# Latent attention: low half of the probabilities on GpSimd, query halves a step later, last score tile before the value matmuls

## What is computed

```python
q_blhd = jnp.einsum('bld,dhk->blhk', x_bld, Wq)
latent_bll = jnp.einsum('bld,dc->blc', x_bld, Wkv_down)
k_blhd = jnp.einsum('blc,chk->blhk', latent_bll, Wk_up)
v_blhd = jnp.einsum('blc,chk->blhk', latent_bll, Wv_up)
attn = jnp.einsum('bqhd,bkhd->bhqk', q_blhd, k_blhd) / jnp.sqrt(jnp.asarray(HD, dtype=x_bld.dtype))
attn = jax.nn.softmax(jnp.where(mask, attn, neg_inf), axis=-1)
y_blhd = jnp.einsum('bhqk,bkhd->bqhd', attn, v_blhd)
return jnp.einsum('bqhd,hdo->bqo', y_blhd, Wout)
```

## Time and profile before

| what | value |
|---|---|
| median of 3 runs | 2997.37 us (2995.15 to 2999.2) |
| profiled execution | 3000.29 us |
| its span on the core | 2998.6 us, mean granted TensorE clock 0.919 |
| busy in the whole span | PE 83%, DVE 72%, ACT 50%, POOL 28% |
| stretch of the latent attention's steps | 1918.66 to 2718 us |

### The profile page before, as it was taken

One profiled execution on the slowest core, in us unless ns is written; L12 is line 12 of the kernel. 1 busy time (PEld: TensorE's weight loads), 2 busy tenths in 40 slices (PEclk: granted clock), 3 DMA queues, 4 the chain that ended last, 5 costly groups with the idle time before them and its releaser, 6 DMA issues. The chain is left out here.

```text
span 2998.6 us, 38823 instructions
## 1 busy us (share of the span) xinstructions
PE 2496.2 (83%) x13889; PEld 1335.8 (45%) x13889; DVE 2165.9 (72%) x3838; ACT 1512.2 (50%) x2213; POOL 841.5 (28%) x820
## 2 busy tenths in 40 slices
PE   6999999999899989899991576688888888885256
PEld 3444444444444444344440344355555555554134
DVE  3389688878889887979107564688878978873765
ACT  5655554546455545555551121377766766772111
POOL 3444343544444434444440000102211211221000
PEclk9999999999999999999995776799999999997678
DMA  5000000000000000000001001000000000001001
GB/s 162 24 1 1 1 1 1 1 1 1 1 1 1 1 1 1 1 1 1 1 1 48 15 1 36 1 2 2 2 3 2 2 3 2 1 2 49 14 1 57
DMA packets 29459, 33.07 MB, mean 11 GB/s; under 512 B 6568, under 2 KB 25704, under 8 KB 29272
## 3 DMA queue, kind: packets, MB, share of 16 engines
q1 hardware_dynamic: 28296, 28.02, 2.9%
q0 software_dynamic: 976, 2.56, 0.3%
HBM read 25.72 MB, written 4.19 MB: 10 GB/s over the span
## 5 line engine op out<-in xcount | busy, mean ns | idle before, releaser
L716 POOL TENSOR_TENSOR g_lo<-g_full,g_hi 128x512 f16<-128x512 f32 x512 | 658.4, 1289 | 912.0 <-ACT g_hi L788 910.4
L788 ACT ACTIVATE g_full<-hid,b_col 128x512 f32<-128x512 f32 x512 | 351.4, 686 | 562.1 <-PE hid L152 560.6
L150 PE MATMUL hid<-y_hi,w_hi 128*128 128x512 f16 x1024 | 396.3, 387 | 37.6 <-DVE y_lo L774 34.9
L151 PE MATMUL hid<-y_lo,w_hi 128*128 128x512 f16 x1024 | 395.7, 386 | 0.0
L152 PE MATMUL hid<-y_hi,w_lo 128*128 128x512 f16 x1024 | 395.2, 386 | 0.0
L150 PE MATMUL acc<-g_hi,w_hi 128*128 128x512 f16 x1024 | 389.2, 380 | 0.0
L151 PE MATMUL acc<-g_lo,w_hi 128*128 128x512 f16 x1024 | 389.1, 380 | 0.0
L152 PE MATMUL acc<-g_hi,w_lo 128*128 128x512 f16 x1024 | 388.9, 380 | 0.0
L788 ACT ACTIVATE g_hi<-hid,b_col 128x512 f16<-128x512 f32 x512 | 348.6, 681 | 0.0
L2027 DVE TENSOR_REDUCE mla_m_col<-mla_ps 128x1 f32<-128x512 f32 (+3 forms) x512 | 225.2, 484 | 66.1 <-PE mla_ps L1869 60.0
L2130 ACT ACTIVATE mla_p_full<-mla_ps 128x1280 f32<-128x1280 f32 x128 | 158.3, 1237 | 143.8 <-PE mla_ps L1899 143.5
(11 more groups left out here) (369 smaller groups left out, 4781.6 us busy)
## 6 DMA issues: line engine op xcount, KB each, us to landing
stage<-in_L_ffn_w_dram SPq DMA_DIRECT2D x16, 512.0 KB, 4.9
x<-in_L_attn_x_dram SPq DMA_DIRECT2D x8, 512.0 KB, 8.4
routed_w<-in_L_ffn_w_dram SPq DMA_DIRECT2D x4, 1024.0 KB, 8.5
out_dram<-x SPq DMA_DIRECT2D x8, 512.0 KB, 5.7
mla_sums<-mla_sum_row SPq DMA_DIRECT2D x128, 2.0 KB
mla_wq<-in_L_attn_Wq_dram SPq DMA_DIRECT2D x1, 1024.0 KB, 6.8
mla_wout<-in_L_attn_Wout_dram SPq DMA_DIRECT2D x1, 1024.0 KB, 9.1
routed_wqkv<-in_L_ffn_wq_dram SPq DMA_DIRECT2D x2, 256.0 KB, 3.7
```

The lines of the kernel that those rows point to most:

```text
L150: pe.matmul(out, w_hi, v_hi, start=first, stop=False)
L151: pe.matmul(out, w_hi, v_lo, start=False, stop=False)
L716: pool.tensor_tensor(g_lo[:, g, :], g_full[:, g, :], g_hi[:, g, :], ALU.subtract).then_inc(tail_done, 1)
L788: act.activation(out[:, g, :], hid[:, ht % 4, :], ACT.Gelu, bias=b1_col[:, ht:ht + 1], scale=1.0 / WS).then_inc(gelu_done, 1)
```

## The change

Four things are changed, all in the steps of the latent attention:

- p_lo = p_full - p_hi goes from VectorE to GpSimd, as the first thing in its step. GpSimd's o_lo and norm columns stand behind it.
- ScalarE writes p_hi first and p_full second, with a semaphore for each (`p_head`, `p_whole`). TensorE's value matmuls do all products with p_hi first (waiting for `p_head`) and the four products with p_lo behind them (waiting for `p_tail`).
- The fourth score tile is issued right behind the key scores, ahead of the value matmuls, and VectorE takes its maximum right behind the other three.
- VectorE makes the query halves of an even step in the odd step behind it, after the maxima, but stays in the even step where the odd one uses bank 6 for a transpose (steps 4, 6 and 8, as long as there is a batch after).

```diff
-                    pe.wait_ge(exp_done, 2 * hn)
+                    pe.wait_ge(p_whole, hn)
...
                 last.then_inc(st_done, 1)
+
+
+            hb, hh, hn = head_of(b, h + LEAD - 2)
+            if exists(hb):
+                pe.wait_ge(s_max, TILES * hn + 1)
+                query_scores(pe, (slot + (h + LEAD - 2) // H) % 2, hh, QUERY_TILES[-1]).then_inc(s_rest, 1)
...
-                pe.wait_ge(p_tail, n + 1)
+                pe.wait_ge(p_head, n + 1)
...
+                own_cols = [slice(KEY_AT[t], KEY_AT[t] + SEQ - t * P) for t in range(TILES)]
                 for t in range(TILES):
-                    out = ps[:, own_bank, t * P:]
-                    cols = slice(KEY_AT[t], KEY_AT[t] + SEQ - t * P)
-                    hi, lo = p_hi[:, h % 2, cols], p_lo[:, h % 2, cols]
+                    out, hi = ps[:, own_bank, t * P:], p_hi[:, h % 2, own_cols[t]]
                     pe.matmul(out, val_hi[:, slot, t, :], hi, start=(t == 0), stop=False)
-                    pe.matmul(out, val_hi[:, slot, t, :], lo, start=False, stop=False)
-                    last = pe.matmul(out, val_lo[:, slot, t, :], hi, start=False, stop=(t == TILES - 1))
+                    pe.matmul(out, val_lo[:, slot, t, :], hi, start=False, stop=False)
+                pe.wait_ge(p_tail, n + 1)
+                for t in range(TILES):
+                    last = pe.matmul(ps[:, own_bank, t * P:], val_hi[:, slot, t, :], p_lo[:, h % 2, own_cols[t]],
+                                     start=False, stop=(t == TILES - 1))
...
+        def turn_bank_used(b, h):
+
+            return exists(b + 1) and h in (*TURN_AT, VALUE_AT)
+
+        def query_halves(dve, b, h):
+
+            hb, hh, hn = head_of(b, h + LEAD)
+            if not exists(hb):
+                return
+            for i in range(2):
+                ring = (hh + i) % RING
+                own = slice(i * LATENT, (i + 1) * LATENT)
+                dve.wait_ge(q_head, hn + i + 1)
+                dve.tensor_copy(q_hi[LATENT:P, ring, :], q_hi[0:LATENT, ring, :]).then_inc(q_twin, 1)
+                if i == 1:
+                    dve.wait_ge(q_twin, hn + i + 1)
+                dve.scalar_tensor_tensor(q_lo[0:LATENT, ring, :], ps[own, 6, :], 1.0 / WS, q_hi[own, ring, :],
+                                         ALU.mult, ALU.subtract).then_inc(q_tail, 1)
...
                 for t in QUERY_TILES[:-1]:
                     query_maxima(dve, hh, t)
+                dve.wait_ge(s_rest, hn + 1)
+                query_maxima(dve, hh, QUERY_TILES[-1])
+            if h % 2 == 1 and not turn_bank_used(b, h):
+                query_halves(dve, b, h - 1)
...
+            if h % 2 == 0 and turn_bank_used(b, h + 1):
+                query_halves(dve, b, h)
...
-                for out in (p_full, p_hi):
+                for out, made in ((p_hi, p_head), (p_full, p_whole)):
                     act.activation(out[:, hh % 2, :], flat[:, 3 * 512:3 * 512 + KEY_COLS], ACT.Exp,
-                                   scale=float(MLA_DIM) ** -0.5).then_inc(exp_done, 1)
+                                   scale=float(MLA_DIM) ** -0.5).then_inc(made, 1)
...
+            hb, hh, hn = head_of(b, h + 1)
+            if exists(hb):
+                pool.wait_ge(p_whole, hn + 1)
+                pool.tensor_tensor(p_lo[:, hh % 2, :], p_full[:, hh % 2, :], p_hi[:, hh % 2, :],
+                                   ALU.subtract).then_inc(p_tail, 1)
```

More of the change, by code:

```diff
@@ L1806, in latent_attention_layer @@
         st_done = sem("st_done")
-        exp_done = sem("exp_done")
+        p_head = sem("p_head")
+        p_whole = sem("p_whole")
         p_tail = sem("p_tail")
@@ L1974, in tensor_step @@
                     pe.wait_ge(x_added, TILES * before + h - OUTPUT_AT)
+                own_cols = [slice(KEY_AT[t], KEY_AT[t] + SEQ - t * P) for t in range(TILES)]
                 for t in range(TILES):
-                    out = ps[:, own_bank, t * P:]
-                    cols = slice(KEY_AT[t], KEY_AT[t] + SEQ - t * P)
-                    hi, lo = p_hi[:, h % 2, cols], p_lo[:, h % 2, cols]
+                    out, hi = ps[:, own_bank, t * P:], p_hi[:, h % 2, own_cols[t]]
                     pe.matmul(out, val_hi[:, slot, t, :], hi, start=(t == 0), stop=False)
-                    pe.matmul(out, val_hi[:, slot, t, :], lo, start=False, stop=False)
-                    last = pe.matmul(out, val_lo[:, slot, t, :], hi, start=False, stop=(t == TILES - 1))
+                    pe.matmul(out, val_lo[:, slot, t, :], hi, start=False, stop=False)
[3 more added lines that the diff above has]
+                                     start=False, stop=(t == TILES - 1))
                 last.then_inc(pv_done, 1)
-            hb, hh, hn = head_of(b, h + LEAD - 2)
-            if exists(hb):
-                pe.wait_ge(s_max, TILES * hn + 1)
-                query_scores(pe, (slot + (h + LEAD - 2) // H) % 2, hh, QUERY_TILES[-1]).then_inc(s_rest, 1)
             hb, hh, hn = head_of(b, h + LEAD)
@@ L2098, in vector_step @@
                                   ALU.subtract).then_inc(val_out, 1)
-            hb, hh, hn = head_of(b, h + LEAD - 2)
-            if exists(hb):
-                dve.wait_ge(s_rest, hn + 1)
-                query_maxima(dve, hh, QUERY_TILES[-1])
-            hb, hh, hn = head_of(b, h + 1)
-            if exists(hb):
-                dve.wait_ge(exp_done, 2 * (hn + 1))
-                dve.tensor_tensor(p_lo[:, hh % 2, :], p_full[:, hh % 2, :], p_hi[:, hh % 2, :],
-                                  ALU.subtract).then_inc(p_tail, 1)
-            hb, hh, hn = head_of(b, h + LEAD)
-            if exists(hb) and h % 2 == 0:
-                for i in range(2):
-                    ring = (hh + i) % RING
-                    own = slice(i * LATENT, (i + 1) * LATENT)
-                    dve.wait_ge(q_head, hn + i + 1)
-                    dve.tensor_copy(q_hi[LATENT:P, ring, :], q_hi[0:LATENT, ring, :]).then_inc(q_twin, 1)
-                    if i == 1:
-                        dve.wait_ge(q_twin, hn + i + 1)
-                    dve.scalar_tensor_tensor(q_lo[0:LATENT, ring, :], ps[own, 6, :], 1.0 / WS, q_hi[own, ring, :],
-                                             ALU.mult, ALU.subtract).then_inc(q_tail, 1)
+            if h % 2 == 0 and turn_bank_used(b, h + 1):
+                query_halves(dve, b, h)
         def scalar_step(act, b, slot, h):
```

## The result

The changed kernel took 3012.3 us in the median (3008.0 to 3014.2), the kernel before 2996.8 on the same chip: a ratio of 1.0048 (1.0036 to 1.0059), slower, where 2962 us was forecast. The profiled execution has a span of 3010.6 us. It is the shortest middle batch of the kernel before, not a typical one: over the six middle batches the mean is 104.4 us before and 108.0 with the change.

The account below looks back on a forecast made before the run. TensorE was taken as nearest the bound, VectorE close behind. Batch steps summed to 97.7 against 101.3 us; with all batches and 4 us of clock, 35 us off 3000.3 gave 2965, median 2962, range 2935 to 2993.

Parts of the forecast that it names:

- Steps 15, 1 and 3: Odd steps that wait for maxima: forecast to go to 4.0, 4.0 and 4.1 us.
- step 4: Its spread waits 1.4 us for ScalarE's evacuations, delayed by the later query halves; the step becomes 6.6 us.
- step 11: Its output waits 0.6 us for the last o_lo behind a p_lo on GpSimd, taking back the step's gain.
- about 2.6 us blocked: Step 8: VectorE's key casts and subtraction run into GpSimd; halves ready at 11.7 us instead of 9, step 9 grows 1.3.
- A: Rival: p_lo on GpSimd takes 4.2 us, so low products stall; kernel slower at 3042 us; chance 0.13.
- B: Rival: GpSimd and VectorE hardly contend for SBUF, so turns and step 9 come earlier; 2930 us; chance 0.15.
- C: Rival: ScalarE's queue eats the gain, every spread step waiting as step 4 does; 2991 us; chance 0.12.
- the signs that I had named: Changed profile: among others p_lo 2.6 to 2.9 us, maxima wait below 1 us per batch, q_lo waits 2 to 3.5 us.
- the next head's score tiles find their bank free; the maxima wait of 7.8 us goes: With p_lo off VectorE, a head's maxima are done about 2.1 us into its step, before score tiles at 3.3.
- the stall at the turns: Steps 5 and 7 keep a stall of about 2 us because the query halves come late; step 9 about 8.1 us.
- step 2: Entered in the batch sum at 5.44 us, its length before the change.
- the clock: The stage's granted clock of 0.98 misses 16 us; some lies next to step 1's vanishing idle time: 4 us gain.

Follow-up runs that it names:

- tile_late_turns: Changed kernel with the fourth score tile and its maximum back behind the value matmuls in steps 5, 7 and 9 only: 2982.7 us, ratio 0.9943.
- fill: Changed kernel with useless 512-column matmuls added between key scores and fourth tile in steps 2, 5, 7 and 9: 2977.9 us, ratio 0.9937.
- polite_alone: Changed kernel with GpSimd's p_lo waiting for VectorE's inverse in step 1 and for the key's halves in step 8: 2985.3 us, ratio 0.9953.
- plo_short: Changed kernel with GpSimd subtracting only 4 of p_lo's 1280 columns, the rest left zero: 2945.0 us, ratio 0.9820.
- inv_early: Changed kernel with the query halves of step 0 kept in step 0, so the inverse follows step 1's maxima directly: 3006.6 us, ratio 1.0027.

## Why the prediction was wrong

**Right.** p_lo takes 2.61 us on GpSimd at its shortest (forecast 2.6 to 2.9). Steps 15, 1 and 3 take 3.93, step 0 5.14, step 4 6.68 with a wait of 0.95 for ScalarE's evacuation (1.4 was forecast), step 8 6.51, step 11 waits 0.45 for o_lo. The hold between the two engines is real, for a whole instruction: the key cast takes 2.84 us instead of 0.41, the 2.4 of "about 2.6 us blocked". Rivals A, B and C didn't happen. Of the signs that I had named, two spoke against me: the wait for maxima is 10.8 us and not below 1, and the turns no longer wait for q_lo.

**The step that failed first** is "the next head's score tiles find their bank free; the maxima wait of 7.8 us goes", worked out for a plain step and applied to all. The fourth tile, moved ahead of the value matmuls, also waits for the step's first maximum. Where the halves stay ahead of the maxima (steps 5, 7, 9) I had put the stall at the turns, 6.65, 6.3 and 8.1 us, with the value matmuls between it and the tile. It came at the tile, ahead of everything: 8.90, 8.49, 9.80. With the tile behind the value matmuls there, the steps took 7.03, 6.65 and 8.12 (`tile_late_turns`), near what my sum described. The misread was in the chain through one bank: I moved the tile and left the value matmuls that had covered its wait out of the reckoning. The 0.5 to 0.6 us that I put down to the maxima in steps 5 and 7 is another wait: the next head's score tiles wait for all four maxima, 0.52 and 0.58 us before, and just as long in `tile_late_turns`.

What the place costs it costs almost wholly through the clock. `fill` has the early tile at full clock and takes 7.22, 6.85 and 8.12 us in these steps, at most 0.2 more than with the late tile; the other 1.64 to 1.68 us of each is half clock.

**Second, step 2** was carried over at 5.44 and took 7.86. I had looked for the hold in steps 4, 6 and 8 but not at the inverse, at the end of step 1, where p_lo now starts 0.9 us ahead of its multiply (1.79 us instead of 0.20). `polite_alone` took 1.24 us of it away, and `plo_short`, without a hold, 1.62. At 6.24 us the step still has a wait of 0.62 for the first maximum, behind the reciprocal and the inverse's products: the place once more.

**Third, the clock** was counted as 4 us of gain, on the ground that idle time goes. It didn't go: TensorE's idle time in the batch is 12.2 us before and 12.3 after, now in fewer and longer pieces, and the clock fell: 34 us of loss (`fill`). This term alone turns the sign: without it the changed kernel is at 2978, below the kernel before.

**The account** per batch, measured less forecast: step 2 +2.4, step 5 +2.2, step 7 +2.2, step 9 +1.7, the rest together -0.8; 105.4 against 97.7. About 5 of these 7.7 us are the clock (105.4 to 100.4 in `fill`), all of them within steps 5, 7 and 9. The range's upper end, 2993, left out a rival in which the waits grow; all three that I had priced were about durations, none about the new order's own wait.

## What to carry to other kernels

An instruction moved ahead of independent work on the same in-order queue loses its cover: ask of each moved instruction what it waits for in every kind of step, not in the plain one. TensorE's waits shouldn't be judged by their sum: 12.2 and 12.3 us of idle time in a batch went with a clock of 1.00 and of 0.95. Their longest isn't a safe sign either: with 3.53 us the clock stayed up in step 9 of `inv_early`, with 1.73 it fell in half of the middle batches of the kernel before. Read the granted clock of each stretch, in more than one batch. And giving GpSimd a long SBUF instruction means finding every SBUF-only instruction of VectorE that can start while it runs; taking one away only exposes the next, while a wait on GpSimd or shorter pieces bounds the loss.
